# Layer 1 of a four-layer kernel: three products in rounded passes, the opening of the recurrence in another order, and four stages behind it joined into one block

## The reference, cut to layer 1

```python
xa = _ln(x, ln1_w, ln1_b)
sx = shift(xa, state) - xa
t = tanh((xa + sx * maa_x) @ maa_w1).reshape(B, L, 5, 32)
mw, mk, mv, mr, mg = einsum('blfd,fdc->blfc', t, maa_w2)
xk, xv, xr, xg = (xa + sx * (maa_j + mj) for j in k, v, r, g)
w = exp(-exp(time_decay + tanh(xw @ decay_w1) @ decay_w2))
r, k, v, g = xr @ Wr.T, xk @ Wk.T, xv @ Wv.T, silu(xg @ Wg.T)
# recurrence over tokens, per head:  out = r (faaaa k v + s);  s = k v + w s
x = x + head_norm(out) * g @ Wo.T
xc = _ln(x, ln2_w, ln2_b);  sxc = shift(xc, state) - xc
rr = sigmoid((xc + sxc * fmaa_r) @ fWr.T)
kk = square(relu((xc + sxc * fmaa_k) @ fWk.T))
x = x + rr * (kk @ fWv.T)
```

## Time and profile before

| | |
|---|---|
| median of three runs | 2617.02 us |
| the profiled execution's own time | 2616.15 us |
| its span (first to last instruction) | 2614.4 us, 1.8 us less than its time |
| mean granted TensorE clock | 0.962 of full speed |
| busy share of the span | TensorE 94%, VectorE 53%, ScalarE 44%, GpSimd 33% |
| DMA | 433 MB, 166 GB/s over the span |

### The profile page before, as it was taken

How to read it: one execution, slowest core, us unless ns; L and a number is a source line. 1 busy time by engine, 2 the same in 40 slices (tenths; PEclk the granted TensorE clock), 3 DMA queues, 4 the chain that set the end, 5 groups by cost and what they waited for, 6 DMA issues and landing times. The chain is left out here.

```text
span 2614.4 us, 37903 instructions
## 1 busy us (share of the span) xinstructions
PE 2450.6 (94%) x13976; PEld 2162.1 (83%) x13976; DVE 1381.7 (53%) x2338; ACT 1143.6 (44%) x2479; POOL 868.9 (33%) x514
## 2 busy tenths in 40 slices
PE   8898899989998789899999999989999999999698
PEld 5676434578995557899999999979998999999698
DVE  4666721388885542332466656534325656664642
ACT  4787421222233331222566666522336666664320
POOL 1100322341122440532355453526226355451300
PEclk9999889999998899999999999999999999999799
DMA  7553362799993356435665556534366666653300
GB/s 237 127 137 75 134 224 76 192 245 241 222 234 133 105 179 222 156 119 182 209 223 185 189 168 200 168 103 164 126 217 214 198 199 191 196 186 88 132 1 26
DMA packets 196348, 432.94 MB, mean 166 GB/s; under 512 B 57820, under 2 KB 92660, under 8 KB 195396
## 3 DMA queue, kind: packets, MB, share of 16 engines
q1 hardware_dynamic: 196164, 430.52, 53.2%
HBM read 332.35 MB, written 106.27 MB: 168 GB/s over the span
## 5 line engine op out<-in xcount | busy, mean ns | idle before, releaser
L2289 PE MATMUL att_ring<-ca_pp,att_arena 128*128 128x400 f32 (+1 forms) x2304 | 433.7, 346 | 10.3 <-issue 8.3
L2289 PEld LDWEIGHTS att_ring<-ca_pp,att_arena 128*128 128x128 f32 (+1 forms) x2304 | 420.0, 189 | 16.5 <-issue 16.3
L2390 POOL TENSOR_TENSOR att_arena<-att_arena 128x1448 fp32r<-128x1448 f32 x64 | 211.8, 3309 | 476.2 <-ACT att_arena L2397 317.7
L2289 PE MATMUL att_ring<-att_arena,qk_wh 128*128 128x362 f32 x1024 | 257.1, 333 | 0.0
L3021 DVE TENSOR_TENSOR ca_yl<-att_ring,att_arena 128x400 fp32r<-128x400 f32 x256 | 146.6, 573 | 193.4 <-ACT att_arena L2982 193.4
L2289 PEld LDWEIGHTS att_ring<-att_arena,qk_wh 128*128 128x128 f32 x1024 | 186.2, 193 | 0.0
L2289 PE MATMUL att_ring<-att_arena,qk_wl 128*128 128x362 f32 x512 | 173.8, 339 | 10.1 <-POOL att_arena L2577 9.3
L2982 ACT ACTIVATE att_arena<-att_ring 128x400 fp32r<-128x400 f32 x256 | 128.8, 503 | 88.5 <-PE att_ring L2289 88.5
L2403 ACT ACTIVATE l_kstage<-att_score,att_shift 100x362 f32<-100x362 f32 x256 | 143.6, 562 | 43.1 <-DVE att_shift L2416 43.1
L1365 ACT ACTIVATE rec_stage<-rec_fbank,rec_columns 128x361 f32<-128x361 f32 x128 | 71.7, 563 | 193.1 <-PE rec_fbank L2289 192.4
L2289 PE MATMUL att_score<-att_arena 128*100 128x362 f32 x768 | 143.8, 337 | 0.8 <-POOL att_arena L2375 0.8
(11 more groups left out here) (410 smaller groups left out, 5960.0 us busy)
## 6 DMA issues: line engine op xcount, KB each, us to landing
att_arena<-ctx_parts SPq DMA_DIRECT2D x64, 1024.0 KB, 5.8
att_arena<-keys SPq DMA_DIRECT2D x64, 724.0 KB, 4.6
att_arena<-ctx_parts SPq DMA_DIRECT2D x64, 420.0 KB, 6.9
keys<-rec_stage SPq DMA_DIRECT2D x32, 724.0 KB, 4.2
keys<-l_kstage SPq DMA_DIRECT2D x32, 724.0 KB, 3.2
l_arena<-kept_value SPq DMA_DIRECT2D x176, 100.0 KB, 5.7
queries<-att_loose SPq DMA_DIRECT2D x64, 200.0 KB, 3.7
att_arena<-queries SPq DMA_DIRECT2D x64, 200.0 KB, 3.0
```

The source lines that it names most:

```text
L2289: issued = nc.tensor.matmul(out, x, y, start=(first and k == 0), stop=(last and k == count - 1))
L2390: self.nc.gpsimd.tensor_tensor(self.kl[:, n % 2].bitcast(F32R), self.kl[:, n % 2], self.kh[:, n % 2].bitcast(F32), ALU.subtract).then_inc( ...
```

## The change

- **Rounded products.** `mix_and_product` is written anew. The k, v and r products and the v and r mixes go through `products` (three passes each); the g mix stays fp32. In `l1r` both the weight and the source are split inside the block, piece by piece; the source of the next product is split while it is made, and `l1s` also splits the next weight. Four mixes are made ahead instead of one. `decay_stage` splits the low-rank activations and `w2`. The weights are first copied from DRAM to DRAM: `load_layer` starts four such copies (`w2`, WkT, WvT, WrT), waits for them, and only then issues its other loads. The four big weights are loaded at the start of `l1d`'s block.
- **Opening of the recurrence.** Weight groups 2 and 3 and the context are asked for ahead of values 3; values 4 and three small matrices go behind the first stores (`EARLY_V` is 1 instead of 2). VectorE takes three of the four low parts of group 1 (`FIRST_LOWS`), between its first rank-1 term and its first scan. ScalarE rounds group g+2 after the first unit of a group instead of after its fourth.
- **One block.** `output_norm_and_gate` replaces `l1z`, `l1b`, `l1f` and `l1g`: batch by batch, output product, norm, transpose, difference, mix, and three batches behind, the gate's product. The sigmoid is done once on all logits at the start of `l1h`. The weight of `l1i` is loaded over the output weight.

```diff
             @block.sync
             def _(sp):
+                loads(sp)
                 product.store(sp, parts, stored)
...
                 if u >= 4:
                     pe.wait_ge(kept, u - 3)
-                terms = product[1](n, half)
-                rows = terms[0][0].shape[-1]
-                for k, (x, y) in enumerate(terms):
-                    last = nc.tensor.matmul(pbank[u % 4][0:rows, :, 0:L], x, y, start=(k == 0), stop=(k == len(terms) - 1))
+                part = slice(n * P, (n + 1) * P)
+                for c in range(CC):
+                    if split_weight and u == 0:
+                        pe.wait_ge(weight_low, c + 1)
+                    if split_source and n == 0:
+                        pe.wait_ge(source_low, CC * half + c + 1)
+                    last = products(nc, pbank[u % 4][:, :, 0:L], [((weight_high_of(c)[:, part], weight_low_of(c)[:, part]),
+                                                                   (source_high_of(half, c), source_low_of(half, c)))],
+                                    first=c == 0, last=c == CC - 1)
                 last.then_inc(full, 1)
+
+            for u in range(MIX_AHEAD):
+                mix(u)
+            for u in range(UNITS):
+                product(u)
+                if u + MIX_AHEAD < UNITS:
+                    mix(u + MIX_AHEAD)
...
+            def low_source(u):
+                half, c = place(u)
+                dve.wait_ge(source_high, u + 1)
+                nc.vector.tensor_tensor(source_low_of(half, c), source_of(half, c), source_high_of(half, c).bitcast(F32),
+                                        ALU.subtract).then_inc(source_low, 1)
...
+            scale(0)
+            if split_weight:
+                for c in range(CC):
+                    low_weight(weight_high_of, weight_low_of, weight_high, c).then_inc(weight_low, 1)
+                    if split_source:
+                        low_source(c)
+            for u in range(UNITS):
+                if next_source and u >= 2:
+                    low_next_source(u - 2)
+                if u:
+                    scale(u)
+                if split_source and 1 <= u <= CC:
+                    low_source(CC + u - 1)
+                if next_weight and u < CC:
+                    low_weight(*next_weight, next_weight_high, u)
+            if next_source:
+                for u in range(UNITS - 2, UNITS):
+                    low_next_source(u)
...
+                half, n = place(u)
                 pool.wait_ge(mix_scaled, u + 1)
-                nc.gpsimd.tensor_tensor(out[:, 4 * half:4 * half + 4, n, :], scaled[:, u % 2],
-                                        cur[:, 4 * half:4 * half + 4, n, :], ALU.add).then_inc(mix_done, 1)
+                dst = scaled[:, u % 2] if next_source else mixed[:, tokens(half), n, :]
+                nc.gpsimd.tensor_tensor(dst, scaled[:, u % 2], cur[:, tokens(half), n, :], ALU.add).then_inc(mix_done, 1)
...
+            if split_source:
+                for c in range(CC):
+                    keep_high_source(CC + c)
+            for u in range(UNITS):
+                half, n = place(u)
+                if next_weight and u < CC:
+                    high_of, low_of = next_weight
+                    nc.scalar.activation(high_of(u), low_of(u).bitcast(F32), ACT.Copy).then_inc(next_weight_high, 1)
+                if next_source:
+                    act.wait_ge(mix_done, u + 1)
+                    nc.scalar.activation(next_source[0](half, n), scaled[:, u % 2], ACT.Copy).then_inc(next_source_high, 1)
                 act.wait_ge(full, u + 1)
-                product[2](act, n, half, pbank[u % 4][0:product[1](n, half)[0][0].shape[-1], :, 0:L]).then_inc(kept, 1)
-
...
+            act.wait_ge(kept, LOW + 2)
+            for high, whole, _ in next_mixing:
+                nc.scalar.activation(high, whole, ACT.Copy).then_inc(next_mix_high, 1)
             for half in HALVES:
...
+            dve.wait_ge(full, DECAY + 2)
+            for i, (high, whole, rest) in enumerate(next_mixing):
+                dve.wait_ge(next_mix_high, i + 1)
+                nc.vector.tensor_tensor(rest, whole, high.bitcast(F32), ALU.subtract)
             dve.wait_ge(parts_stored, 16 * stored_count)
...
-    EARLY_V = 2
+    EARLY_V, FIRST_LOWS = 1, 3
...
                 sp.dma_start(columns[:, i], head_columns[i]).then_inc(columns_in, 16)
             load_weights(2)
+            load_weights(3)
             load_values(2)
+            load_context(1)
             load_values(3)
-            load_context(1)
-            load_weights(3)
             load_key(1)
-            load_values(4)
             load_rest(1)
             sp.dma_start(now[:, 0], present[:, 0]).then_inc(now_in[0], 16)
-            for tile, src in later:
-                sp.dma_start(tile, src).then_inc(later_in, 16)
...
                 store(step)
+                if step == 1:
+                    for tile, src in later:
+                        sp.dma_start(tile, src).then_inc(later_in, 16)
...
-                if b == 0 and h == G3 - 1 and g + 2 < GROUPS:
+                if b == 0 and h == 0 and g + 2 < GROUPS:
                     high_weights(g + 2)
...
                 if b == 0 and g and h == 0:
-                    pe.wait_ge(fweight_low, CC * (g - 1) + c + 1)
+                    if g == 1 and c < FIRST_LOWS:
+                        pe.wait_ge(first_low, c + 1)
+                    else:
+                        pe.wait_ge(fweight_low, CC * (g - 1) + c + 1 - FIRST_LOWS)
...
             rank1(0)
+            dve.wait_ge(fweight_high, 1)
+            for c in range(FIRST_LOWS):
+                nc.vector.tensor_tensor(fwl[1][:, c].bitcast(F32R), fwl[1][:, c], fwh[1][:, c].bitcast(F32), ALU.subtract).then_inc(first_low, 1)
             scan(0)
             rank1(1)
             multiply(0)
...
+def output_norm_and_gate(nc, prefix, X, ident, ahead, out_weight, out_weight_in, gate_weight, gate_weight_in, next_weight, z, y, diff, squares,
+                         before, logits, norm_scale, norm_offset, mix_gate, mix_key, eps, parts, moves):
+
+    RING_Z, RING_R = 2, 3
+    Z_AHEAD, R_BEHIND, TURN_BEHIND = 2, 3, 1
+    ROUND_AT = {0: 1, 3: 2, 5: 3}
+    PIECES_AT = {0: ((0, 0), (0, 1)), 1: ((0, 2), (1, 0)), 2: ((1, 1), (1, 2)), 4: ((2, 0), (2, 1)), 5: ((2, 2),),
+                 6: ((3, 0), (3, 1)), 7: ((3, 2),)}
+    KEY_MIX_AT = {6: (0, (0, 1)), 7: (0, (2, 3)), B + 1: (1, (0, 1, 2, 3))}
...
+            tile, source, arrived = next_weight
+            sp.wait_ge(out_low, CC)
+            sp.dma_start(tile, source).then_inc(arrived, 16)
+            moves(sp)
...
+            for n in range(B + R_BEHIND):
+                if n == 0:
+                    first_output(zbank[0][0:L, :])
+                elif n < B:
+                    output(n)
+                if n == B:
+                    turn(B - 1)
+                if n >= R_BEHIND:
+                    gate(n - R_BEHIND)
+                if 1 <= n < B:
+                    turn(n - 1)
...
+                if 0 <= n - 2 < B:
+                    affine(n - 2)
+                    high_gate_source(n - 2)
+                if n + Z_AHEAD < B:
+                    high_source(n + Z_AHEAD)
+                if n < 2:
+                    for c in range(2 * n, 2 * n + 2):
+                        nc.scalar.activation(gh[:, c, :], gate_weight[:, c, :], ACT.Copy).then_inc(gate_high, 1)
+                if n < B:
+                    act.wait_ge(var_ready, n + 1)
+                    nc.scalar.activation(std[:, n:n + 1], vareps[:, n:n + 1], ACT.Sqrt).then_inc(std_ready, 1)
+                if n in ROUND_AT:
+                    parts.round(act, ROUND_AT[n])
+                if n >= R_BEHIND:
+                    keep_logits(n - R_BEHIND)
...
+            for n in range(B + 2):
+                if 0 <= n - 2 < B:
+                    low_gate_source(n - 2)
+                if n + Z_AHEAD < B:
+                    low_source(n + Z_AHEAD)
+                for b, t in PIECES_AT.get(n, ()):
+                    parts.subtract(pool, b, t)
...
+            for n in range(B + 2):
+                m = n - 2
+                if m >= 0:
+                    difference(m)
+                    dve.wait_ge(diff_done, 2 * (m + 1))
+                    dve.wait_ge(z_full, m + 1)
+                    for c in range(CC):
+                        mix(slice(m, m + 1), mix_gate, z, c).then_inc(mixed, 1)
+                if n < B:
+                    add(n)
+                if n < 2:
+                    for c in range(2 * n, 2 * n + 2):
+                        low_weight(gh, gl, gate_weight, gate_high, gate_low, c)
+                if n < B:
+                    normalise(n)
+                if n in KEY_MIX_AT:
+                    half, columns = KEY_MIX_AT[n]
+                    for c in columns:
+                        mix(slice(half * B // 2, (half + 1) * B // 2), mix_key, squares, c).then_inc(squares_done, 1)
...
```

(24 more changed lines are left out.)

296 lines of the change are left out of this document (235 added, 61 removed).

## The result

The changed kernel took 2595.47 us (median of four runs, 2592.95 to 2598.06), the kernel before beside it 2618.72: a ratio of 0.9912 with a 95% interval of 0.9895 to 0.9929, a gain of 23 us (19 to 27). The forecast was 2582 with a range of 2568 to 2600. The sign and the range hold; the time lies outside the forecast's own case (2574 to 2591) and nearer to the rivals.

A forecast was written before the change was run, and what follows sets the result against it. TensorE, busy nearly all the time, was taken as the bound. Gains of 16.9 (products), 7 (opening) and 10.5 (block), 34.4 us in all, took the profiled 2616.15 to 2581.8, given as 2582 us; range 2568 to 2600.

The forecast's parts named there:

- the forecast's own case: Whole kernel: a time of 2574 to 2591 us, given 65%.
- Three product stages: `l1r`, `l1s`, `l1u`: rounded passes replace fp32 products, net gain 16.9 us (bounds 11 to 18), to about 28, 25, 26 us.
- the clock rival: Product stages and joined block: waits keep TensorE at the lower clock, a pass costs 0.364 us, kernel 2665 us; 3%.
- Opening: Start of the recurrence: new load order removes TensorE's waits for GpSimd and ScalarE; gain 7 us, bounds 1 and 12.
- The rival of late values: Recurrence opening: the stall moves in full to VectorE, gain 1 us instead of 7, kernel 2589 us; 12%.
- One block: Four stages behind the recurrence joined: 66.2 us against 76.7, 10.5 us gained (bounds 5 and 14).
- TensorE leads, but not at the two ends: Joined block: TensorE's 6.0 us per batch sets the pace, above 4.5 on VectorE and about 4.5 on ScalarE.
- TensorE waiting for GpSimd in the joined block: Joined block: a sign named beforehand that would show the forecast wrong; no size given.
- Contention: Joined block: VectorE and GpSimd slow each other beside GpSimd's 32 us of subtractions; 3 us added.
- VectorE and GpSimd take turns: Joined block: the pair's 4.7 plus 2.0 us paces each iteration, gain 5 us, kernel 2588 us; 12%.
- Before layer 1: DRAM copies ahead of SP's loads: loads start at 305 instead of 291, still before their reader; cost nothing.
- The sigmoid and the weight over the output weight: `l1h`: 5 to 6 us of ScalarE hide under 21 us of matmuls, the weight has 60 us to arrive; nothing.

## Why the prediction came out as it did

- **The whole.** The profiled execution lies 12.1 us above the 2581.8 of the sum: 6.2 from the block, 3.0 from the products, 1.7 from the copies, 2.1 from `l1h` and `l1i`, 0.5 from the lines between, and -1.4 from the code that the change doesn't touch. The sum had the copies, `l1h` and `l1i` at nothing.
- **Three product stages: mechanism right, the terms too small.** `l1r` took 28.1 of 28, by luck: in four of the eight programs with the same stage it took 30.6 to 30.9, the longer start at the lower clock that the prediction had as its bound ("up to 4.5"). `l1s` and `l1u` missed by 2.0 and 1.6 us. Each has 3.4 us at the lower clock right behind its start (0.94 on the mean), which costs 1.7 us and which the sum had at none; the clock rival had been weighed for whole stages only. The mix was priced at 0.55 us; that is right in a row of mixes, but between products it takes 3.13 - 2.18 = 0.95.
- **Opening: right but for one sign.** 6.9 us against 7, fourth sum at 47.8 against 47 (47.3 to 49.9 over the ten programs with this order, 54.1 to 56.6 over the three with the old one), TensorE's idle time at the sums ended by VectorE, with values 2 landing late (3.78 us at the second sum). But "no wait of ScalarE for a store" did not hold: ScalarE waits 9.3 us for one, until 525.90. It ended no idle time of TensorE, which was waiting for the second sum meanwhile. From 496 to 545:

```profile
PE rec_sum L1489 <- DVE rec_work L1548: 4.5, 2, 3.8
ACT rec_stage L1447 <- DMA keys<-rec_stage: 9.3, 1, 9.3
```

  The rival of late values showed only as those 3.8 us. What its full price would have been no run shows; the reverse order, with group 3 late instead, cost 6.4 us.
- **One block: the step that failed** and cost most is "TensorE leads, but not at the two ends", with "six iterations with all three parts, at 6.0 and small waits: 38 us". From the first copy: output 3 began at 16.8 us (15.2 in the sum), gate product 5 was done at 60.9 (53.2), the last logits kept at 71.7 (62.3 without the 3 us for contention). So 1.6 + 6.1 + 1.7 us more, less those 3 and 0.3 at the exit: 6.1 us over. The prediction counted each engine's work per batch, 4.5 us on VectorE and on ScalarE, and found it under TensorE's 6.0. It didn't follow the order on the two across an iteration: the next addition behind a mix, that behind an affine step, that behind a keep and a rounding, 6.78 us in a ring. Reordering ScalarE brought 6.3 us back, 3.8 in the loop and 4.6 in the tail, less 2.1 at the head. The second part of the step is the clock: the sum priced every gate product at full clock, and gate products 5 and 7 took 4.5 us instead of 3.0 behind waits of 5.17 and 2.92 us. The prediction's remark that the joined block could lose a few us at its ends by the clock came true, and it had no term in the sum. Its sign of being wrong, TensorE waiting for GpSimd in the joined block, came too (0.6 to 0.8 us in an iteration, 2.92 in the tail), at the end of the ring and not through GpSimd's own work.
- **Contention: right in kind, small in size.** 3 us were allowed; taking away the context's subtractions for three of four batches gave 4.7 (GpSimd's busy time fell from 36.6 to 23.6 us). The rival "VectorE and GpSimd take turns", at 12%, gave the block's time nearly exactly (5 us gained, 4.3 measured), but by luck: its cause is the smaller part of it (4.7 us alone, the order 6.3).
- **Before layer 1: the copies were put at nothing and cost some 2 us.** The sum had looked only at whether the loads are in before their reader; they are. The step that failed is that the stores queued behind SP's wait, "which nobody reads in this block", cost nothing: the end of the block waits for their landing, and the last one lands 1.8 us later on the mean. The sign given for it, `l1d` 4 us behind the last store, came out at 5.3. Why that store is slower is open.
- **The sigmoid and the weight over the output weight: nothing, as said.** `l1h` took 25.7 us in the run with the block alone, 25.5 before, and 26.2 in the changed kernel.

## What to carry to other kernels

Where several engines pass a batch round, work per engine and batch is a lower bound only: write down the order of each engine and look for a ring (an instruction of the next batch behind one that waits for another engine), for it sets the pace even when each engine is a quarter idle. A keep of a finished result belongs behind the step that the others wait for, above all in the last iterations, where its own input is late. A wait of a few us can cost twice, as the wait and as the lower clock seen behind it here; price both, and where two edits shorten one wait, run them together too. And before work is moved to an engine that is idle elsewhere, follow its buffers and stores as well as its time.

## Not expected of the hardware

- A VectorE operation with two SBUF inputs of four columns took 1.25 us beside a GpSimd subtraction and 0.16 alone. In the row at 859.43 it ended at 860.68 and GpSimd's two subtractions at 860.65: here what contention cost went by the operation that it met, not by its own size. One of the normalisation's form (one SBUF tensor, two columns) took 965 ns on the mean beside GpSimd and 662 with most of the subtractions gone.
- Three passes of 32 rows cost 0.95 us between products of 128 rows and 0.55 in a row of their own: 0.28 us from the last pass of one kind to the next, where 0.18 is the pace.
- The clock fell for 3.4 us behind the start of `l1s` in all nine programs with rounded products and single mixes, four ahead or one, in none of the three with the stage of before, and in neither of the two with the mixes in pairs, though within `l1s` the pairs lie behind the place where it fell (the stage ahead has them too). The reason is open: ahead of the fall TensorE was idle for the 0.85 us between the stages, and so it was in the two with pairs and in the kernel before, where the clock didn't fall.
